# Sorting rows to experts: an indirect gather per tile from a permutation inverted on TensorE, with gate and residual added in sorted order

## The reference

```
h = layernorm(x) * (1 + ca) + sa
x = x + ga * attention(h)         # 16 heads of width 8, a recurrence over 256 steps with a state of 8x8
h = layernorm(x) * (1 + cb) + sb
x = x + gb * ffn(h)

ffn(x): route = softmax(x @ router_w + router_b)         # 8 experts
        e = argmax(route) of each row
        y = (silu(a) * g) @ w2[e],  a, g = split(x @ w1[e])    # 128 -> 2*512 -> 128
        return y * max(route)
```

## Time and profile before

| | us |
|---|---|
| median of 3 timed runs | 517.53 (517.5 to 519.65) |
| span of the profiled execution | 543.5 |
| PE busy / DVE busy | 389.4 / 414.1 |
| ACT busy / POOL busy | 272.0 / 276.2 |
| mean granted clock of TensorE | 0.840 of full speed |

### The profile page before, as it was taken

How to read it: one execution, slowest core, us unless ns; L and a number is a source line. 1 busy time by engine, 2 the same in 40 slices (tenths; PEclk the granted TensorE clock), 3 DMA queues, 4 the chain that set the end, 5 groups by cost and what they waited for, 6 DMA issues and landing times. The chain is left out here.

```text
span 543.5 us, 8910 instructions
## 1 busy us (share of the span) xinstructions
PE 389.4 (72%) x2643; PEld 352.1 (65%) x2643; DVE 414.1 (76%) x1196; ACT 272.0 (50%) x600; POOL 276.2 (51%) x323
## 2 busy tenths in 40 slices
PE   2957555969677799450968664879999338999980
PEld 1322115969677699450968663879999238999980
DVE  5679999996999978999998996685957013548733
ACT  2688749663144244554555461453755026555620
POOL 1174329699999674537379375002223743232430
PEclk9988775868977787975889776789999759999996
DMA  8367859900000009203100012024130111233205
GB/s 206 60 70 122 117 105 144 113 1 1 0 2 1 0 8 378 82 0 50 29 2 0 1 35 60 20 39 99 41 107 25 55 54 40 77 91 94 60 29 159
DMA packets 50205, 35.01 MB, mean 64 GB/s; under 512 B 10992, under 2 KB 46608, under 8 KB 50032
## 3 DMA queue, kind: packets, MB, share of 16 engines
q1 hardware_dynamic: 47152, 29.07, 27.5%
q0 software_dynamic: 3008, 5.40, 3.2%
HBM read 15.26 MB, written 10.27 MB: 47 GB/s over the span
## 5 line engine op out<-in xcount | busy, mean ns | idle before, releaser
L570 PE MATMUL bank<-prod_o,ID 128*128 128x128 f32 x512 | 85.5, 336 | 41.3 <-POOL prod_o L287 18.0
L921 POOL DMA_INDIRECT placed_y<-Q,place x46 | 44.1, 958 | 126.0 <-ACT Q L1226 60.6
L570 PEld LDWEIGHTS bank<-prod_o,ID 128*128 128x128 f32 x512 | 79.9, 246 | 43.1 <-POOL prod_o L287 18.8
L718 PE MATMUL bank<-Q,p 128*128 128x128 f32 x736 | 96.5, 280 | 0.0
L718 PEld LDWEIGHTS bank<-Q,p 128*128 128x128 f32 x736 | 91.6, 196 | 0.1
L280 POOL TENSOR_TENSOR prod_o<-Q,ST 128x1024 f32<-128x1024 f32 x28 | 62.5, 2231 | 42.4 <-PE bank L574 29.1
L1063 ACT ACTIVATE p<-S,GAM 128x64 f32<-128x64 f32 x126 | 47.6, 410 | 70.6 <-DVE S L1498 68.0
L1219 ACT ACTIVATE p<-big 128x1024 f32 x46 | 48.5, 1057 | 54.8 <-PE bank L718 36.9
L1498 DVE TENSOR_REDUCE S<-p 128x64 f32<-128x320 f32 x126 | 55.4, 474 | 6.5 <-ACT p L1063 6.0
L1485 DVE TENSOR_REDUCE U<-p 128x32 f32<-128x288 f32 x128 | 52.7, 439 | 0.2 <-DVE p L1479 0.2
L1479 DVE TENSOR_TENSOR p<-S,bank 128x256 f32<-128x256 f32 x128 | 49.2, 407 | 0.7 <-ACT bank L1058 0.7
(11 more groups left out here) (225 smaller groups left out, 786.7 us busy)
## 6 DMA issues: line engine op xcount, KB each, us to landing
big<-in_L_ffn_w_dram SPq DMA_DIRECT2D x1, 4096.0 KB, 13.1
big<-big SPq DMA_DIRECT2D x16, 192.0 KB, 4.5
Q<-sorted_h SPq DMA_DIRECT2D x46, 64.5 KB, 2.0
sorted_h<-ZERO SPq DMA_DIRECT2D x2, 1472.0 KB, 16.4
X<-in_L_attn_x_dram SPq DMA_DIRECT2D x8, 256.0 KB, 4.8
big<-big SPq DMA_DIRECT2D x16, 128.0 KB, 4.9
X<-Q SPq DMA_DIRECT2D x32, 64.0 KB, 2.4
K<-placed_y SPq DMA_DIRECT2D x8, 256.0 KB, 3.0
```

What stands on the lines that cost most here:

```text
L570: pe.matmul(ps, ID[:, :], prod_o[:, k % 2, i, :], start=(i == 0), stop=False, skip_group_check=True)
L718: m = pe.matmul(bank[(1, 6)[g % 2] + k][:, c * P:(c + 1) * P], W1E[g % 2][:, f:f + P], XST[:, g % 3, :], start=True, stop=True)
L921: pool.indirect_dma_start(placed_y[g // NF], bass.IndirectOffsetOnAxis(ap=place[:, g:g + 1], axis=0), YS[:, g % YR, :], None).then_inc(sem ...
```

## The change

sorted_h and placed_y go. A table rows_h in DRAM has a row of 385 values for each row of a slice: h2 (128), the highest probability (1), x1 (128) and the gate gb (128), and one spare row. SP writes it: the gates early, straight from DRAM to DRAM, x1 and h2 when they are there (`store_x1`, `store_rows`). Instead of scattering rows to places, the kernel inverts the permutation: DVE splits each row's place into a tile number (hi) and a partition (lo), makes one-hot matrices of both (`one_hots`), with the row's number in place of the one, and PE multiplies them and sums over the 16 blocks (`invert`). What comes out is, for each tile and partition, the row's number in rows_h and in the output; empty places get the spare row and a number past the end (`indices`). POOL gathers each tile with one indirect DMA of 128 rows of 385 values (`gather`), seven tiles ahead at the start, then one after each scatter. DVE multiplies y by probability and gate while it reads PSUM (`gate_y`), adds x1 (`add_x1`), and POOL scatters the tile straight into the output, with a bounds check that leaves out the empty places (`scatter`). ACT no longer copies y, and its exponential of the second slice is moved from iteration 22 to 13. `probability` moves from iterations 3 and 25 into the recurrence and into iteration 15. Not shown in the diff: the constants that POOL writes at the start (iotas of 128, 16 and twice 16 values, for ZERO and the spare places), and `invert(1)` on PE after second(13) in iteration 15.

```
@@ -61,27 +62,24 @@
     AT_ROUTE, AT_SORT = AT_SHIFT + 4, AT_SHIFT + 5
     G_ATTEND, G_TURN = 9, 10
     F_ROUTE = F_TURN[1] + 2
-    MOVE = 7
-    SCAT = F_ROUTE - 2
-    YIN = 12
-    YACT = F_ROUTE + 1
     NF = NT + E - 1
-    NFE = NF * P
     D1 = D + 1
-    sorted_h = [nc.dram_tensor(f"sorted_h{s}", (NFE, D1), F32, kind="Internal").ap() for s in range(NTIME)]
-    placed_y = [nc.dram_tensor(f"placed_y{s}", (NT * P + NFE, D), F32, kind="Internal").ap() for s in range(NTIME)]
+    RD = D1 + 2 * D
+    SPARE = NT * P
+    rows_h = [nc.dram_tensor(f"rows_h{s}", (SPARE + 1, RD), F32, kind="Internal").ap() for s in range(NTIME)]
+    rows_t = [rows_h[s][0:SPARE, :].rearrange("(b p) e -> p b e", p=P) for s in range(NTIME)]
     gate_h = nc.dram_tensor("gate_h", (B * D,), F32, kind="Internal").ap()
-    out_t = out.rearrange("b (s p) d -> s p b d", p=P)
+    out_rows = out.rearrange("b n d -> (b n) d")
@@ -163,14 +161,16 @@
         ex = RT[:, 768:896].rearrange("p (t e) -> p t e", t=NT)
-        ZERO = sb("ZERO", [P, D])
         texf = sb("texf", [P, NF])
-        PLACES = texf
         posf = sb("posf", [P, NT])
-        place = sb("place", [P, 2 * NF], U32)
-        maxp = [sb(f"maxp{h}", [P, NT]) for h in range(NHALF)]
+        lo, hi = y2, lmx
+        UNIT = sb("UNIT", [P, P])
+        FROM = sb("FROM", [P, NT])
+        TO = sb("TO", [P, NTIME, NT])
         tex = [sb(f"tex{h}", [P, NF], I32) for h in range(NHALF)]
-        pos = [sb(f"pos{h}", [P, NT], U32) for h in range(NHALF)]
+        idx = [sb(f"idx{h}", [P, 2, NF], U32) for h in range(NHALF)]
+        OHT = sm[:, 0:3, :].rearrange("p a t -> p (a t)")[:, 0:NT * 2 * NF].rearrange("p (t x j) -> p t x j", t=NT, x=2)
...
@@ -220,7 +217,10 @@
         flatq = [Q_[h][:, :, :].rearrange("p t d -> p (t d)") for h in range(NHALF)]
-        XS = flatq[0][:, 0:XR * D1].rearrange("p (r d) -> p r d", r=XR)
+        flatw = [PD[h][:, :, :].rearrange("p d t -> p (d t)") for h in range(NHALF)]
+        XS = [tile[:, r * RD:(r + 1) * RD] for tile in (flatq[0], *flatw) for r in range(2)]
+        XS.append(ST[1][:, :, :, :, :].rearrange("p r k n v -> p (r k n v)")[:, 0:RD])
         XST = flatq[1][:, 0:3 * P].rearrange("p (r d) -> p r d", r=3)
...
@@ -289,17 +290,15 @@
-        def load_y(queue, s, q):
...
+        def store_rows(queue, s, h):
+            queue.wait_ge(sem("h2_evac"), 4 * s + 2 * (h + 1))
+            queue.wait_ge(sem("maxp_set"), NHALF * s + h + 1)
+            queue.dma_start(rows_t[s][:, HB * h:HB * (h + 1), 0:D1], H2[s][h][:, :, :]).then_inc(sem("rows_in", s), 16)
+        def store_x1(queue, s):
+            queue.wait_ge(sem("x1_ready", s), 4)
+            queue.dma_start(rows_t[s][:, :, D1:D1 + D], XG[s]).then_inc(sem("rows_in", s), 16)
@@ -455,10 +454,13 @@
             for s in range(NTIME):
-                rows = sorted_h[s].rearrange("(n p) d -> p n d", p=P)
-                sp.dma_start(rows[:, :, 0:D], ZERO[:, :].unsqueeze(1).broadcast_to([P, NF, D])).then_inc(sem("padded", s), 16)
-                    sp.dma_start(rows[:, :, D:D1], PLACES[:, :].unsqueeze(2)).then_inc(sem("padded", s), 16)
+                for start in range(0, RD, P):
+                    size = min(P, RD - start)
+                    sp.dma_start(rows_h[s][SPARE:SPARE + 1, start:start + size], ONES[0:1, 0:size]).then_inc(sem("rows_fixed", s), 16)
+            sp.wait_ge(sem("gates_out"), 16)
+            for s in range(NTIME):
+                sp.dma_start(rows_h[s][0:SPARE, D1 + D:RD].rearrange("(b t) d -> b t d", b=B),
+                             gate_h.rearrange("(b d) -> b d", b=B).unsqueeze(1).broadcast_to([B, P, D])).then_inc(sem("rows_fixed", s), 16)
@@ -468,30 +470,16 @@
-            for g in range(NTIME * NF):
...
+            for s in range(NTIME):
+                if s == 1:
+                    for h in range(NHALF):
+                        move_outputs(sp, 1, [h])
+                store_x1(sp, s)
+                for h in range(NHALF):
+                    store_rows(sp, s, h)
+            for r in range(YR):
+                sp.wait_ge(sem(f"ys_out{r}"), 16 * len(range(r, NTIME * NF, YR)))
...
@@ -660,9 +648,19 @@
+            def invert(s):
+                for t in range(NT):
+                    if t % 4 == 0:
+                        pe.wait_ge(sem("ohp_ready"), 4 * s + t // 4 + 1)
+                    m = pe.matmul(RANK_BANK[s][:, 0:2 * NF], OHP[:, t, :], OHT[:, t, :, :].rearrange("p x j -> p (x j)"), start=(t == 0), stop=(t == NT - 1))
+                m.then_inc(sem("inv_ps"), 1)
             for g in range(NG):
+                if g == PG:
+                    invert(0)
                 if g - 1 == W_AT[0]:
...
@@ -728,7 +726,7 @@
                 if g >= 1:
-                    pe.wait_ge(sem("ys_ready"), g)
+                    pe.wait_ge(sem("y_gated"), g)
                 for c in range(FC):
...
@@ -850,23 +853,29 @@
-            def place_rows(s):
...
+            def gather(g):
+                s, j = divmod(g, NF)
+                if j == 0:
+                    pool.wait_ge(sem("idx_ready"), 2 * (s + 1))
+                    pool.wait_ge(sem("rows_in", s), 16 * (NHALF + 1))
+                    pool.wait_ge(sem("rows_fixed", s), 16 * 5)
                     if s == 0:
-                        pool.wait_ge(sem("prod_ready", h), NG // 2 + 1)
-                    else:
-                        pool.wait_ge(sem("sqo_used"), 2)
-                    pool.iota(H2[s][h][:, :, D:D1], [[P, HB], [0, 1]], base=h * HB * P, channel_multiplier=1,
-                              allow_small_or_imprecise_dtypes=True).then_inc(sem("place_set"), 1)
-                pool.wait_ge(sem("place_set"), NHALF * (s + 1))
-            def sort_rows(s):
-                pool.wait_ge(sem("pos_ready"), s + 1)
-                pool.wait_ge(sem("h2_evac"), 4 * (s + 1))
-                pool.wait_ge(sem("padded", s), 32)
-                for t in range(NT):
-                    pool.indirect_dma_start(sorted_h[s], bass.IndirectOffsetOnAxis(ap=pos[s][:, t:t + 1], axis=0),
-                                            H2[s][t // HB][:, t % HB, :], None).then_inc(sem("scattered", s), 16)
+                        pool.wait_ge(sem("weights_in"), NHALF)
+                        pool.wait_ge(sem("ot_in0_0"), 16 * HB)
+                        for h in range(NHALF):
+                            pool.wait_ge(sem("prod_ready", h), PG)
+                if g >= XR:
+                    pool.wait_ge(sem("ys_ready"), g - XR + 1)
+                pool.indirect_dma_start(XS[g % XR], None, rows_h[s],
+                                        bass.IndirectOffsetOnAxis(ap=idx[s][:, 0, j:j + 1], axis=0)).then_inc(sem(f"xs_in{g % XR}"), 16)
+            def scatter(g):
+                s, j = divmod(g, NF)
+                pool.wait_ge(sem("ys_ready"), g + 1)
+                pool.indirect_dma_start(out_rows, bass.IndirectOffsetOnAxis(ap=idx[s][:, 1, j:j + 1], axis=0), YS[:, g % YR, :], None,
+                                        bounds_check=B * N - 1, oob_is_err=False).then_inc(sem(f"ys_out{g % YR}"), 16)
...
@@ -915,15 +921,12 @@
+            for g in range(XR):
+                gather(g)
             for g in range(NTIME * NF):
-                pool.wait_ge(sem("ys_ready"), g + 1)
-                pool.wait_ge(sem("place_ready"), g + 1)
-                pool.indirect_dma_start(placed_y[g // NF], bass.IndirectOffsetOnAxis(ap=place[:, g:g + 1], axis=0),
-                                        YS[:, g % YR, :], None).then_inc(sem(f"ys_out{g % YR}"), 16)
-                if g == 0:
-                    place_rows(1)
-                if g == SCAT:
-                    sort_rows(1)
+                scatter(g)
+                if g + XR < NTIME * NF:
+                    gather(g + XR)
@@ -1218,13 +1221,6 @@
-            def ys(g):
-                act.wait_ge(sem("y_ps"), g + 1)
-                if g >= YR:
-                    act.wait_ge(sem(f"ys_out{g % YR}"), 16 * (g // YR))
-                act.activation(YS[:, g % YR, :], bank[3][:, 0:D], ACT.Copy).then_inc(sem("ys_ready"), 1)
@@ -1243,12 +1239,9 @@
                     copy_w1(g + 2)
-                if 2 <= g < YACT + 2:
-                    ys(g - 2)
                     root(sd[:, :], ve[:, :])
-                if g == NF - 1:
+                if g == F_ROUTE:
                     exponentials(1)
@@ -1545,8 +1538,9 @@
                 dve.wait_ge(sem("lexp"), s + 1)
-                link(dve.tensor_reduce(posf[:, :], ex[:, :, :], AX_X, ALU.add))
-                link(dve.reciprocal(maxp[s][:, :], posf[:, :]))
+                yield from settle(dve.tensor_reduce(lm[:, :], ex[:, :, :], AX_X, ALU.add))
+                for h in range(NHALF):
+                    dve.reciprocal(H2[s][h][:, :, D:D1], lm[:, h * HB:(h + 1) * HB].unsqueeze(2)).then_inc(sem("maxp_set"), 1)
@@ -1577,8 +1571,30 @@
                 yield from settle(dve.tensor_reduce(posf[:, :], t8[:, :, :], AX_X, ALU.add))
```

(64 more changed lines are left out.)

73 lines of the change are left out of this document (12 added, 61 removed).

## The result

The changed kernel takes **550.5 us** (549.16 to 551.75, four runs) against 518.59 (517.5 to 520.34): ratio 1.060, interval 1.055 to 1.065. Slower was forecast, but 521.5 and not 550.5, above the whole range.

What follows compares the result with a forecast made beforehand. The prediction took DVE to bound the recurrence, PE the experts' stage and a chain the tail. From 517.5, terms -11 - 0.7 + 5.7 + 0.3 + 2.7 + 7.0 - 1.0 + 1 = +4.0 gave 521.5 us, range 512 to 532.

Steps and rivals of the forecast that it cites:

- What bounds before: Whole kernel: DVE bounds the recurrence, PE the experts, a chain the tail; 25 us of profile stalls absent from timed runs.
- Rival B: Stalls beside POOL's scatter bursts are real in timed runs and the change gives some back; 10 of 25 gives 511; chance 0.17.
- Recurrence and start: Up to the first tile: new DVE one-hots and probability cost +5.7, indices and first gathers +0.3.
- First slice: Experts' loop, slice one: DVE evacuates every y and adds x1, exposed in some iterations, +2.7 (1 to 4).
- Second sorting: Iterations 14 and 15: DVE's one-hots, then PE's 3.9 us inversion starting with their first quarter, delay later tiles, +7.0 (5 to 9).
- Rival C: DVE's additions are absorbed better, with second sorting 5 because its quarters overlap: 515.5 to 519.5; chance 0.18.
- Supply: Experts' tiles: gathers landing in 2.9 almost use up the 3.05 us of cover, +1 (0 to 12).
- the seam: Between the slices and at the finish: DVE's multiplications of placed_y go, which had delayed PE, -1.0.
- Rival A: Tile supply: gathers land in 4.0, so the period is 3.3 instead of 2.8, +12, giving 533; chance 0.20.
- Tail: End of kernel: last YS row needs only one DVE addition and one scatter, ending at 532.4 instead of 543.5, -11.

Runs made afterwards that it cites:

- e7: Kernel before, with each scatter of the second burst waiting until the one ahead of it has landed: 553.9 us, ratio 1.017.
- e9: Kernel before, with the second burst of scatters in pairs, every second scatter waiting until those ahead have landed: 543.8 us, ratio 0.995.
- e8: e6 plus a POOL drain right behind its last gather: 542.6 us, ratio 0.992; where the kernel before takes 518.3, 530.9 us, ratio 1.023.
- e10: e8 with POOL issuing each gather ahead of the scatter: 524.2 us, ratio 1.011, where before takes 518.3; 541.0, ratio 0.989, where before takes 545.8.
- e5: Changed kernel with the second slice's one-hots, still in one lump, moved from iteration 14 to 15: 560.7 us, ratio 1.024.
- e6: Changed kernel with second-slice one-hots spread over iterations 15 to 18, inversion in 18, and stores of x1 and rows cut into quarters: 548.8 us, ratio 1.006.
- e1: Changed kernel with second-slice one-hots spread over iterations 15 to 18, inversion and indices in 18 and 19: 560.5 us, ratio 1.024.
- e3: Changed kernel with POOL issuing each gather ahead of the scatter: 559.45 us, ratio 1.023.
- b_before: Kernel before, unchanged, run again for a profile on the second group's chip: 547.0 us, one run.

## Why the prediction was wrong

*What bounds before: right for the runs, wrong in its reason.* "The timed runs have no room for these stalls" holds on the 518 chips (spans 515.6 to 519.0). The prediction took the profiled execution for a disturbed one. The hold-ups are lasting on other chips, in timed runs as well, and POOL's unbroken issues are what brings them at the second burst (e7, e9; the first was not tried). Rival B had the mechanism. On those chips it moved the ratio from 1.06 to 1.035, not to below 1, because the changed kernel loses 16 us of its own there. A part of that lies beside unbroken issues; why gathers come up to 2 us late in the rest is not shown. That the forecast was set against 518, and was then measured on such a chip, was luck: the profile it read was not of that kind.

*Recurrence and start: right.* Forecast 6.0, measured 4.5, and 3.7 to 5.6 over the four profiles on 518 chips with this part alike.

*First slice: mis-sized by a missing step.* 2.7 forecast, 5.9 measured. With the quartered store, e8 and e10 take 65.2 from turn 0 to 17 on a 518 chip where the changed kernel takes 71.2, so the store cost 6.0 there (4.9 by the table above), and what is left is 1.0 above before. DVE's gating was over-priced, and the sentence that SP's new stores "lie beside the recurrence" is the step that failed. It is true of slice one alone. x1 and rows of slice two are stored in the middle of the experts' loop, while gathers are under way, and the prediction has no term for them.

*Second sorting: the largest miss.* 7.0 forecast, 18.2 measured for the stretch, 1.5 of it at turn 21 (under supply). The failed step is "it can begin with the first quarter of the one-hots at 419.6". Between hidden(15) and the inversion stands second(13), the product with W2 for tile 13, which waits for gate_y(12); before, it waited there for a copy of y on ACT. In DVE's program gate_y(12) is behind the whole lump. So DVE's 5 us and PE's inversion add up instead of overlapping, and behind the wait the clock is low and stretches second, inversion and next tile by about 6 us (6.90 - 3.9, 2.07 - 1.06, twice about 0.9). Even with the overlap it would not have been 7.0: in e5 the inversion does begin with the first one-hots, and turns 17 to 18 still take 11.8 more than a tile. The granted clock is 0.62 from 424 to 433 us there, and a fall of the clock while PE waits had no term either. The price of the inversion itself, 3.9, was right at the full clock (3.88 in e6, 3.67 in e1). With the lump spread and the stores in quarters, stretch 17 to 22 takes 21.0, 7.1 over before; that this is the 7.0 of the forecast is luck, since the forecast got there by an overlap that did not happen. Rival C had this stretch at 5 by the same overlap, and falls with it.

*Supply: right to name it, wrong in weight.* Forecast 1 with bound 12, measured about 7.5 with the seam: turns 22 to 45 take 74.8, and 67.3 once the gathers go first (e10). The landing is 3.2 (median of after) where 3.05 was allowed, and 2.9 taken. The Trainium skill (DMA: Bandwidth & Descriptors, Anatomy of one DMA) gives an estimate of 2.5, under all of them; the trace does not agree, no gather of after landed in less than 3.0. A few tenths over the cover cost 4.8 us in tiles 29 to 45 (476.4 to 526.9, 50.5 us, where before has 45.7), and at the seam 2.1 more; 1.28 us of earlier issue brought it all back. Rival A named this mechanism with a landing of 4.0 and a period of 3.3; the period was 3.16. The 4.9 us wait at tile 10 is the same thin cover beside a store. The 1.3 at tile 21 has no store of SP's beside it; its gather took 4.1 us to land, and why is not shown.

*Tail: the gain that did not come.* -11 forecast, -2.4 measured. The end was worked out as last scatter plus landing, 2.5. The step that failed is "The end comes at 529.9 + 0.3 + 2.2": the earlier trace rows stop at the last scatter and at the load that waits for it, and leave out that POOL's program is not over. Its drain ended 4.9 us before the end of before. It counts as no work in the busy groups, and it lay under a longer chain, but it was the next thing to be late once that chain went. Without it the last scatter's landing would have ended the run at 541.8, a gain of 10.2, near the 11. With an early drain stretch 45 to the end takes 16.8 in e8 and 17.6 in e10 (both on the 518 chip), a gain of 8.3 and 7.5.

*Why slower at all, even mended.* e10 is 5.9 above before on a 518 chip, 5.5 in its span: +5.5 to turn 0, +1.0, +7.1 for the inversion and the tiles around it, -0.6, -7.5. PE and DVE bound their stages, and the change gives both new work there; what it takes away lay on SP's and POOL's queues and in the tail.

## What to carry to other kernels

Before pricing what a removed tail gives back, list what ends under it, the sequencers' last instructions too. For a lump of new work on an in-order engine, ask which small instruction behind it another engine is waiting for, and cut the lump. A transfer whose cover is used up to a tenth of a microsecond pays for every store that is moved beside it, so cut and pace the stores, and issue ahead of other DMAs the one that is waited for (6.7 us on a 518 chip, next to nothing on a 546 chip).

## What the runs showed of the hardware

POOL's drain at the end, counted from its last issue, took 7.8 us after 94 DMAs, 8.3 after 101, 8.9 after 108 and 1.4 to 1.5 after 7: about 0.074 us for each DMA since the last drain, plus 0.9. Its record is 8.94 to 8.95 long in all five profiles with 94 and 10.10 in all ten with 108. An earlier drain under other work takes most of it off the end.

On some chips, an unbroken run of POOL's indirect DMAs (0.96 each, 0.30 between) makes DVE, ACT and PE stand with nothing that they wait for: 1.5 us after four in a row (e3), some 20 us beside nineteen (before, b_before). With a break of 1.6 to 2.1 us after each two it does not happen (e9). On other chips twelve in a row did nothing visible (after, 454 to 469 us). What is blocked there, and why chips differ, stays open. The prediction thought of the loading of instructions: from 418 to 438 us the instruction queues carried one transfer in b_before and three in e7, but engines that stand also need fewer, so this decides nothing.

Gathers of 128 rows of 1540 bytes land in 3.0 to 4.1 us with no store of SP's beside them, 3.2 in the median, and in 8.1 beside a store of 1 MB in 512-byte pieces (after, tile 10).
